# Attention scores from packed pairs of groups on one Trainium2 core: selection products ahead of and beside the loop, and half of every second copy on ScalarE

## The reference

```python
qkv = x @ Wqkv + bqkv
q, k, v = jnp.split(qkv, [D, D + KV], axis=-1)
q = q.reshape(b, s, H, HD)
k = jnp.tile(k.reshape(b, s, G, HD), (1, 1, H // G, 1))
v = jnp.tile(v.reshape(b, s, G, HD), (1, 1, H // G, 1))
scores = jnp.einsum('bqhd,bkhd->bhqk', q, k) / HD
prob = jax.nn.softmax(scores, axis=-1)
out = jnp.einsum('bhqk,bkhd->bqhd', prob, v).reshape(b, s, D)
return out @ Wout + bout
```

## Time and profile of the kernel before

| what | value |
|---|---|
| median of 3 runs | 1158.87 us (1155.47 to 1159.03) |
| the profiled execution | 1158.44 us |
| its span, first to last instruction | 1156.7 us |
| busy share of the span: PE, DVE, ACT, POOL | 87%, 76%, 49%, 60% |
| attention, products of keys to the last residual | 16.5 to 154.8 us of the span |

### The profile page before, as it was taken

How to read it: one execution, slowest core, us unless ns; L and a number is a source line. 1 busy time by engine, 2 the same in 40 slices (tenths; PEclk the granted TensorE clock), 3 DMA queues, 4 the chain that set the end, 5 groups by cost and what they waited for, 6 DMA issues and landing times. The chain is left out here.

```text
span 1156.7 us, 13476 instructions
## 1 busy us (share of the span) xinstructions
PE 1004.1 (87%) x3956; PEld 631.6 (55%) x3956; DVE 882.0 (76%) x1134; ACT 564.7 (49%) x1191; POOL 696.7 (60%) x493
## 2 busy tenths in 40 slices
PE   5899967999999999996859886989789887686898
PEld 2577755888888888873424422433344333232477
DVE  4588736777777777776568889978989799999862
ACT  1666632344434434433655766564745575464141
POOL 2256620565656565550369787988889789989100
PEclk9899987999999999997969998999889999899999
DMA  3000024433442453313134454544346455554001
GB/s 109 1 1 0 1 89 117 129 105 93 119 138 84 110 139 99 96 50 96 48 100 130 149 157 142 138 145 129 125 140 154 120 132 148 161 141 139 1 1 37
DMA packets 60592, 116.07 MB, mean 100 GB/s; under 512 B 10832, under 2 KB 15952, under 8 KB 60416
## 3 DMA queue, kind: packets, MB, share of 16 engines
q1 hardware_dynamic: 59408, 113.63, 34.5%
q10 hardware_dynamic: 1136, 1.90, 0.5%
HBM read 113.99 MB, written 1.51 MB: 100 GB/s over the span
## 5 line engine op out<-in xcount | busy, mean ns | idle before, releaser
L1432 POOL TENSOR_TENSOR uB<-u,rows_B 128x512 f32<-128x512 f32 x256 | 319.6, 1273 | 37.0 <-DVE da L1582 34.3
L796 POOL TENSOR_TENSOR lutw<-lutw,lt 128x865 f32<-128x865 f32 x80 | 187.3, 2341 | 162.2 <-DVE lt L773 156.4
L1600 PE MATMUL ya<-hV,ident 128*128 128x512 f32 x336 | 195.0, 667 | 79.0 <-DVE hV L1524 78.6
L1582 DVE TENSOR_TENSOR_SCAN da<-da,uB 128x512 f32<-128x512 f32 x168 | 201.1, 1220 | 35.6 <-ACT da L1511 30.8
L1600 PEld LDWEIGHTS ya<-hV,ident 128*128 128x128 f32 x336 | 62.4, 204 | 179.8 <-DVE hV L1524 141.1
L1441 POOL TENSOR_TENSOR hP<-hS,rows_C 128x512 f32<-128x512 f32 x88 | 111.9, 1271 | 37.0 <-DVE hS L1579 19.4
L1579 DVE TENSOR_TENSOR_SCAN hS<-da,uB 128x512 f32<-128x512 f32 x88 | 106.7, 1213 | 20.2 <-ACT da L1511 9.9
L1510 ACT ACTIVATE da<-zero 128x2 f32<-128x2 f32 x256 | 43.1, 169 | 146.9 <-DVE hV L1524 145.5
L1524 DVE TENSOR_TENSOR hV<-da,rows_C 128x512 f32<-128x512 f32 x168 | 112.4, 670 | 0.0
L751 ACT ACTIVATE ah<-ups 128x1024 fp32r<-128x1024 f32 x40 | 41.2, 1029 | 121.7 <-DVE ups L769 121.7
L1600 PE MATMUL ya<-hP,ident 128*128 128x512 f32 x176 | 94.1, 617 | 0.0
(11 more groups left out here) (292 smaller groups left out, 2108.2 us busy)
## 6 DMA issues: line engine op xcount, KB each, us to landing
rows_B<-bc_rows SPq DMA_DIRECT2D x128, 256.0 KB, 3.5
rows_C<-bc_rows SPq DMA_DIRECT2D x128, 256.0 KB, 4.3
wr<-in_moe_w SPq DMA_DIRECT2D x41, 384.0 KB, 4.3
cwb<-cw_rows SPq DMA_DIRECT2D x16, 512.0 KB, 4.1
cwb<-cw_rows SPq DMA_DIRECT2D x16, 384.0 KB, 4.7
cwb<-cw_rows SPq DMA_DIRECT2D x16, 256.0 KB, 3.9
lut_f<-in_lut_idx SPq DMA_DIRECT2D x1, 2160.0 KB, 9.0
cwb<-cw_rows SPq DMA_DIRECT2D x16, 128.0 KB, 3.6
```

What stands on the lines that cost most here:

```text
L796: e.tensor_tensor(part, part, lt[:, q, :], ALU.add).then_inc(s_la, 1)
L1432: e.tensor_tensor(uB[:, n % UBUF, :], u[:, seg % 2, d, :], RB[:, q, :], ALU.mult).then_inc(s_ub, 1)
L1582: e.tensor_tensor_scan(a[:, way], a[:, way], uB[:, n % UBUF, way], 0.0, ALU.mult, ALU.add).then_inc(s_sc, 1)
L1600: return e.matmul(ya[n % 2][:, :], g.ident[:, :], at, start=False, stop=False, skip_group_check=True).then_inc(done, 1)
```

## The change

Scores take two products for a unit instead of four. `qs` and `kk` now hold, for a pair of groups, all four combinations of rounded part and rest in 128 rows: two groups by 16 dimensions by four. These rows are made on PE, by products with 0/1 matrices (`selq`, `selk`, cut from the identity by POOL): 20 pieces of 512 columns, two products each, into four banks in turn. With the values' products (one more piece, number 11) they make the list `pieces` of 21. ACT empties even pieces and DVE odd ones; a piece of keys is written twice, each time for one group of the pair by the factors in `only`. Pieces 0 to 9 (tokens 0 to 511) are made ahead of the loop, the others in its steps 0 to 4, on each engine after that step's scores, maximum or ahead of its exps. Keys and queries are computed once, not doubled on the host, so two sets of query products take the place of four. Both blocks become one. `copy_queries` goes from ACT to POOL and copies 1024 columns instead of 512. For odd units, DVE copies only the first half of the turned probabilities, and ACT the second (`second_copy`), after that step's `exps`. The mask gmask is gone.

```diff
+PAIRS = GROUPS // 2
...
-    s_vc, s_pn = c.counters("at_", "vc pn", nc.gpsimd)
+    s_vc, s_pn, s_qc = c.counters("at_", "vc pn qc", nc.gpsimd)
...
-    s_ex, s_oe, s_qc = c.counters("at_", "ex oe qc", nc.scalar)
+    s_ex, s_oe, s_pa = c.counters("at_", "ex oe pa", nc.scalar)
...
+        qs = c.sb(ctx, "qs", [P, PAIRS, HJ, T], F32R)
+        kk = c.sb(ctx, "kk", [P, PAIRS, 2, T], F32R)
...
+        qh, ql = (c.sb(ctx, n, [P, KC, T], F32R) for n in ("qh", "ql"))
+        kh, kl = (c.sb(ctx, n, [KV, T], F32R) for n in ("kh", "kl"))
...
+        selq = c.sb(ctx, "selq", [P, 2, KC * PAIRS, P], F32R)
+        selk = c.sb(ctx, "selk", [KV, 2, PAIRS, P], F32R)
+        only = c.sb(ctx, "only", [P, 2])
...
+        pieces = [("k", p, h) if j is None else ("q", p, h, j) for h in range(NH)
+                  for j in [None] + list(range(HJ)) for p in range(PAIRS)]
+        FIRST = len(pieces) // NH
+        pieces.insert(FIRST + 1, ("v",))
+        BANKS = [ops[:, :], mps[:, :], tps[:, 0, :, :].rearrange("p g q -> p (g q)"),
+                 tps[:, 1, :, :].rearrange("p g q -> p (g q)")]
+        PER_STEP = [range(FIRST, FIRST + 3)] + [range(FIRST + 1 + 2 * i, FIRST + 3 + 2 * i) for i in range(1, 5)]
+        assert PER_STEP[-1][-1] == len(pieces) - 1
+        kps = tps[0:KV, :, :, :].rearrange("p k g q -> p (k g q)")
+        qps = [sps[:, i, :, :].rearrange("p g q -> p (g q)") for i in range(KC)]
...
+                e.memset(selq[:, :, :, :].bitcast(F32), 0.0).then_inc(s_z, 1)
+                e.memset(selk[:, :, :, :].bitcast(F32), 0.0).then_inc(s_z, 1)
                 e.memset(vcur[:, :, :, :], 0.0).then_inc(s_vz, 1)
+                e.wait_ge(s_z, 2)
+                for part in range(2):
+                    for again in range(2):
+                        to = selk[:, part, :, :].rearrange("p r (a s d) -> p r a s d", a=2, s=4)
+                        e.tensor_copy(to[:, :, :, 2 * part + again, :], g.ident[0:KV, 0:KV].rearrange(
+                            "p (r a d) -> p r a d", a=2, d=HD)).then_inc(s_se, 1)
+                for part in range(2):
+                    for again in range(2):
+                        to = selq[:, part, :, :].rearrange("p r (a s d) -> p r a s d", a=2, s=4)
+                        e.tensor_copy(to[:, :, :, 2 * again + part, :], g.ident[:, :].rearrange(
+                            "p (r a d) -> p r a d", a=2, d=HD)).then_inc(s_se, 1)
+                e.wait_ge(wt.at_in, wt.at_n)
+                e.tensor_tensor(g.x[:, :, :], g.x[:, :, :],
+                                wt.bout[:, :].unsqueeze(1).broadcast_to([P, NB, D]), ALU.add).then_inc(s_xb, 1)
...
+                def copy_queries(n, u, s):
+                    qb, j = divmod(u, HJ)
+                    if j == 0:
+                        if isinstance(n, int):
+                            e.wait_ge(s_ea, (FIRST + 1) // 2)
+                            e.wait_ge(s_ed, FIRST // 2)
+                        e.wait_ge(s_sc, START + n - HJ)
+                        e.tensor_copy(qcur[:, :, :, qb * P:(qb + 1) * P],
+                                      qs[:, :, :, bass.ds(s * SEQ + qb * P, P)].bitcast(F32)).then_inc(s_qc, 1)
...
+                def pack(t):
+                    what, at = pieces[t][0], BANKS[t % 4]
+                    if t >= 4:
+                        e.wait_ge(s_ed if t % 2 else s_ea, (t - 4) // 2 + 1)
+                    if what == "v":
+                        for n in range(NB):
+                            for k in range(KC):
+                                mm = e.matmul(at[:, n * KV:(n + 1) * KV], g.feat[:, k, n * P:(n + 1) * P],
+                                              wt.wv[:, k, :], start=k == 0, stop=k == KC - 1)
+                    elif what == "k":
+                        _, p, h = pieces[t]
+                        e.matmul(at, selk[:, 0, p, :], kh[:, half(h)], start=True, stop=False)
+                        mm = e.matmul(at, selk[:, 1, p, :], kl[:, half(h)], start=False, stop=True)
+                    else:
+                        _, p, h, j = pieces[t]
+                        i, r = j // KC, j % KC * PAIRS + p
+                        if h == 0:
+                            e.wait_ge(s_ql, i + 1)
+                        e.matmul(at, selq[:, 0, r, :], qh[:, i, half(h)], start=True, stop=False)
+                        mm = e.matmul(at, selq[:, 1, r, :], ql[:, i, half(h)], start=False, stop=True)
+                    mm.then_inc(s_pk, 1)
+
+                e.wait_ge(wt.at_in, wt.at_n)
+                rows(kps, wt.wk).then_inc(s_k, 1)
+                for i in range(KC):
+                    rows(qps[i], wt.wq[:, :, i * P:(i + 1) * P]).then_inc(s_q, 1)
+                e.wait_ge(s_se, 8)
+                e.wait_ge(s_kl, 1)
+                for t in range(FIRST):
+                    pack(t)
...
-                    for gg in range(0, GROUPS, 2):
-                        for i, k in enumerate((kh, kl)):
-                            mm = e.matmul(sps[:, u % 2, gg:gg + 2, :], qcur[:, j, qb * P:(qb + 1) * P],
-                                          k[:, gg:gg + 2, bass.ds(s * SEQ, SEQ)], start=i == 0, stop=i == 1)
+                    for p in range(PAIRS):
+                        mm = e.matmul(sps[:, u % 2, 2 * p:2 * p + 2, :], qcur[:, p, j, qb * P:(qb + 1) * P],
+                                      kk[:, p, :, bass.ds(s * SEQ, SEQ)], start=True, stop=True)
...
                 def turn(n, u, s):
                     e.wait_ge(s_pn, START + n + 1)
                     e.wait_ge(s_pe, START + n)
+                    if u % 2 == 0:
+                        e.wait_ge(s_pa, START + s * (U // 2) + u // 2)
...
                     e.wait_ge(s_pe, START + n + 1)
+                    if u % 2:
+                        e.wait_ge(s_pa, START + s * (U // 2) + u // 2 + 1)
...
+                    if isinstance(b, int) and b == 0:
+                        for t in PER_STEP[i] if i < len(PER_STEP) else ():
+                            pack(t)
+                        if i == TURN:
+                            e.wait_ge(s_ea, (len(pieces) + 1) // 2)
+                            e.wait_ge(s_ed, len(pieces) // 2)
...
+                def unpack(t):
+                    what, at = pieces[t][0], BANKS[t % 4]
+                    if t % 2 == 0:
+                        return
+                    e.wait_ge(s_pk, t + 1)
+                    if what == "v":
+                        e.tensor_tensor(v[:, :, :], at.rearrange("p (n w) -> p n w", n=NB),
+                                        wt.bv[:, :].unsqueeze(1).broadcast_to([P, NB, KV]), ALU.add).then_inc(s_ed, 1)
+                    elif what == "k":
+                        _, p, h = pieces[t]
+                        for a in range(2):
+                            i = e.tensor_scalar(kk[:, p, a, half(h)], at, only[:, a:a + 1], None, ALU.mult)
+                        i.then_inc(s_ed, 1)
+                    else:
+                        _, p, h, j = pieces[t]
+                        e.tensor_copy(qs[:, p, j, half(h)], at).then_inc(s_ed, 1)
+
...
+                e.wait_ge(s_kh, 1)
+                e.scalar_tensor_tensor(kl[:, :], kps, wt.bk[0:KV, 0:1], kh[:, :].bitcast(F32), ALU.add,
+                                       ALU.subtract).then_inc(s_kl, 1)
+                for i in range(KC):
+                    e.wait_ge(s_qh, i + 1)
+                    e.scalar_tensor_tensor(ql[:, i, :], qps[i], wt.bq[:, i:i + 1], qh[:, i, :].bitcast(F32), ALU.add,
+                                           ALU.subtract).then_inc(s_ql, 1)
+                e.wait_ge(s_ma, 4)
+                for t in range(FIRST):
+                    unpack(t)
...
-                    e.tensor_copy(pT[:, u % 2, :, :, :], tps[:, :, :, :]).then_inc(s_pe, 1)
+
+                    kbs = slice(0, QB - u % 2)
+                    e.tensor_copy(pT[:, u % 2, kbs, :, :], tps[:, kbs, :, :]).then_inc(s_pe, 1)
...
+                e.wait_ge(s_k, 1)
+                e.activation(kh[:, :], kps, ACT.Identity, bias=wt.bk[0:KV, 0:1]).then_inc(s_kh, 1)
+                for i in range(KC):
+                    e.wait_ge(s_q, i + 1)
+                    e.activation(qh[:, i, :], qps[i], ACT.Identity, bias=wt.bq[:, i:i + 1]).then_inc(s_qh, 1)
+                e.wait_ge(s_ma, 4)
...
+                def second_copy(n, u, s):
+                    if u % 2:
+                        e.wait_ge(s_pt, START + n + 1)
+                        e.wait_ge(s_pv, START + n - 1)
+                        e.activation(pT[:, u % 2, 1, :, :], tps[:, 1, :, :], ACT.Copy).then_inc(s_pa, 1)
...
-                    if at := unit(b, i, 0):
-                        copy_queries(*at)
+                    for t in PER_STEP[i] if isinstance(b, int) and b == 0 and i < len(PER_STEP) else ():
+                        unpack(t)
                     if at := unit(b, i, SCORES):
                         exps(*at)
+                    if at := unit(b, i, TURN):
+                        second_copy(*at)
```

(55 more changed lines are left out.)

40 lines of the change are left out of this document (19 added, 21 removed).

## The result

The change makes the kernel slower: 1164.39 us (median of 6 runs, 1162.19 to 1165.31) against 1157.86 us for the kernel before (6 runs, 1153.81 to 1159.69). The ratio is 1.0059, with a 95% interval of 1.0038 to 1.0080.

The account below looks back on a forecast made before the run. The prediction took PE to bound the attention loop. Start 0.3, six turns 4.2, drain 0.5 and one clock fall 1.1 made +6.1 on 1158.4: 1164.5 us, range 1156 to 1171.5.

Parts of the forecast that it names:

- up to unit 6: From the start to unit 6 of the attention: between -0.5 and +2 us, taken as +0.3 us.
- six turns: Loop between units 6 and 30: six four-unit turns of 13.6 against 12.88 us, +4.2 us (+2.5 to +5.5).
- one fall of the clock: PE's clock in the loop: one fall to half speed beyond today's, +1.1 us (0 to +8).
- drain: After the last unit's maximum: turn(28) 1.36 late, 0.3 and 0.5 given back, together +0.5 us.
- The new path: Attention loop: closed path through turn(24) waiting for ACT's copy behind exps(26), sum 13.68, taken as 13.6 against 12.88 us.
- The new step: Attention loop, maximum(26) to turn(24): 1.32 + 1.82 + 0.73 = 3.87 us, where before it is 2.51.
- The third rival: Attention loop: the clock falls in every turn, six falls instead of one, 1171 us; chance 0.13.
- both cancel: Start and loop: packing keeps first units at 2.4 GHz, worth 2; turns only 0.5 longer; 1160 us, chance 0.28.
- Ahead of the loop: Projections and packing before the first scores: scores(0) starts at 41.5 us, against 41.86 in the kernel before.
- sign of being right: Start of the attention: first scores at 41 to 42 us, one of the listed signs of a right forecast.
- The rival that the packing stalls PE: Start: if ACT or DVE needs over 0.9 us a piece, start 3 to 5 us later, 1168 us; chance 0.05.
- The first rival: Attention loop: ACT's half copy is never waited for, turns 1.0 to 1.4 us shorter, 1151.5 us; chance 0.12.

Follow-up runs that it names:

- e1: The changed kernel with ACT's second half copy placed ahead of that step's exps instead of behind it: 1150.71 us, 0.9948 of the kernel before.
- e5: The changed kernel, ACT's order unchanged, with DVE doing the residual after the next maximum instead of ahead of it: 1156.96 us, 0.9993 of the kernel before.
- e4: The kernel before with the half copies alone, placed ahead of exps on ACT: 1153.96 us, 0.9970 of the kernel before.
- e3: The kernel before with the half copies alone, placed behind exps on ACT as in the change: 1166.43 us, 1.0084 of the kernel before.
- e2: The changed kernel without ACT's half copies, DVE copying every unit whole: 1153.54 us, 0.9960 of the kernel before.
- e6: The changed kernel with the copy of the queries back on ACT instead of POOL: 1164.94 us, 1.0056 of the kernel before.
- e7: e1 with the values' products moved from place 11 to place 17 of the pieces: 1148.83 us, 0.9914 of the kernel before.

## Why the prediction was right

**The number.** 1164.5 was forecast against 1164.39, +0.5% against +0.59%. To be that close is luck in part: single runs spread by 3 us, and errors of the steps cancel. The steps count, here against the two profiled executions, whose attention grew by 5.94 us.

| step | forecast | measured |
|---|---|---|
| up to unit 6 | +0.3 | +0.64 (59.30 to 59.94) |
| six turns, clock at 2.4 GHz | +4.2 | +3.6 (below) |
| one fall of the clock | +1.1 | +1.05 |
| drain | +0.5 | +0.61 (17.64 to 18.25 from maximum(30) to the end) |
| behind the attention | 0 | +0.8 (1001.87 to 1002.63, within what profiles differ by) |

**The new path** was right in place and size: the turn of every fourth unit (20, 24, 28) waits for ACT's copy of the unit before, queued behind the exps that the residual made late. Its sum was 13.68 by the rows and 13.6 by choice; five of the six turns took 13.51 to 13.62. The 4.2 was 0.6 too large by the other end of the subtraction: I took 12.88 for every turn of before, but its first took 13.31, so 6 x 12.88 was 0.6 short. The new step, from the late maximum to the turn behind ACT's copy, was put at 3.87 and measured 3.81 (115.40 to 119.21). e1 to e5 show the cause: the copy's place in ACT's queue (e1, and e4 against e3), the copy itself (e2), and the residual that makes exps late (e5).

**The clock.** Stretches of the kernel after:

```profile
42.50:52.70 10.20, 6.21 (x30) 4.33 (x28) 7.41 (x12) 9.41 (x31) 4.48 (x3) 1.00 0.00 1
73.00:77.10 4.10, 2.19 (x26) 1.39 (x25) 3.59 (x7) 2.89 (x14) 3.56 (x4) 1.00 0.00 0
77.10:80.50 3.40, 3.23 (x25) 2.49 (x26) 1.23 (x1) 2.04 (x10) 1.81 (x1) 0.50 0.00 0
80.50:84.00 3.50, 3.50 (x33) 2.84 (x33) 1.89 (x3) 2.15 (x8) 1.82 (x2) 1.00 0.03 7
```

The first of these stretches in the kernel before:

```profile
42.50:52.70 10.20, 8.63 (x24) 6.08 (x23) 5.49 (x8) 7.52 (x29) 4.20 (x3) 0.50 0.00 1
```

The loop of e6:

```profile
59.00:143.00 84.00, 67.48 (x700) 47.86 (x699) 59.34 (x89) 61.78 (x221) 47.20 (x29) 1.00 0.00 1
```

In the kernel after, the granted clock fell once in the loop, for 3.4 us at 1.2 GHz, behind a stretch of 4.1 us in which PE worked 2.19 and stood idle for 2.08 before turn(8). That turn of the loop took 14.66 in place of 13.6: a fall costs 1.05, as forecast. The third rival, a fall in every turn, did not come: one in six here, and none in e6, whose pauses are the same (2.1 to 2.2 us, but for the first of 1.4). That I counted one and one came is luck: nothing here says which pause brings a fall, and e6, without one, has the same time (1.0056 of before, the change 1.0059). The Trainium skill, "TensorE: Matmul & The Clock Gate", section "HAM oscillation — how this bites in real kernels", describes waits for DMAs of some 3 to 5 us, each with its fall. Those are longer than the pauses here, so it does not say that every turn here would have one; with these shorter pauses a fall was the exception.

**The rival "both cancel"** was right in its first half. The first units kept 2.4 GHz (1.00 over 42.5 to 52.7, against 0.50 before). It did not help: unit 6 was still 0.64 later. PE did only 6.21 us of work in these 10.2, so its speed was not what held them up; the first exps (45.99, before 44.71) waited for ACT, with its pieces and its table load. The forecast had this order too, but exps at 45.0.

**Ahead of the loop** I had scores(0) at 41.5; it was 42.5, 0.6 later than before, and outside the 41 to 42 that I had named as a sign of being right. The steps that slipped are small ones: the queries' products ended 0.3 later, the keys' piece costs DVE 1.40, not 1.3, and PE reached the values at 37.10, not 36.4.

```profile
32.46 1.40 DVE L498 TENSOR_SCALAR kk<-mps,only 128x512 fp32r<-128x512 f32 x2
...
37.10 3.79 PE L396 MATMUL tps<-wv,feat 128*128 128x64 f32 x32
...
37.46 1.04 POOL L352 CAST qcur<-qs 128x1024 fp32r<-128x1024 f32 x1 [13.70 <-DVE qs L502]
...
42.50 0.63 PE L426 MATMUL sps<-kk,qcur 128*128 128x512 f32 x2
...
44.70 1.28 ACT L590 ACT_TABLE_LOAD   x1
...
45.99 0.47 ACT L590 ACTIVATE prob<-sps,mx 128x256 f32<-128x256 f32 x1
```

POOL's copy of the queries took 1.04 us, inside the bounds of 0 and 1.89 and well hidden. The rival that the packing stalls PE did not come: a piece of queries took ACT 0.60 us and DVE 0.69, and only the keys' pieces (1.26 and 1.40) were over 0.9; the longest that PE stood idle between the pieces ahead of the loop was 0.75.

**The first rival** (nobody waits for ACT's half) was priced at 1151.5 (its own terms, -1.1 x 6 - 0.5, give 1151.3), and e1, which makes it true by another way, the order of two calls, has 1150.7. The total is close, but its terms were not: a turn became shorter by 0.81 (12.98 to 12.17), not by 1.1, and 1.3 came from the start (maximum(6) at 58.02, before 59.30), most of it the keys' products (5.32 us in e1, 6.42 in the profile of before).

## What to carry to other kernels

When a piece of work moves to an engine with time to spare, its place in that engine's queue decides, not the engine's busy share: here ACT was busy half of the time, and PE waited for the copy some 2 us in every turn, since it stood behind an instruction that itself waits for the slowest part of the loop. Put the short helper whose inputs are ready ahead of the long step that has to wait, and give the sum as a closed path through the loop, not as saved work by engine: DVE had 8 us less to do and PE 5.5, and the kernel took 6.5 us more. In a start-up, work on PE that is needed late belongs into PE's first forced gap (e7).

## What was not expected

- e1 and e2 came out 3 us faster than their expectations. Their profiles show where the attention gained besides the turns: the drain was shorter (18.25 to 16.63 in e1, 17.65 in e2), maximum(6) came 1.9 and 0.9 earlier, and neither has the change's fall of the clock (1.05).
- A product with 64 rows of contraction is no quicker than one with 128: selections from `selk` and from `selq` both start 0.23 us apart at 2.4 GHz in the change's timeline.
- A float32 product costs nearly four times a float32r one, not twice, as "two passes" may suggest. It shows as two records, but the 16 products of the queries took 13.90 us at a granted clock of 1.00, 0.87 each, against 0.23 from start to start for a float32r product of the same 512 columns.
- Moving the values' products (e7) kept 3.3 of 3.7 us. How much of the rest e7 could still give, and how often the clock falls at a pause of 2.2 us in runs that were not profiled, stays open.
